# State scan in pairs of states, and a counting stage with the additions first

## What is computed

```python
e = leaky_relu(s_src[src] + s_tgt[tgt], 0.2)          # attention logits, one per edge and head
attn = exp(e - max(e)) / segment_sum(...)[tgt]
agg = segment_sum(proj[src] * attn, tgt)              # sum over a node's edges
deg = segment_sum(ones, src)                          # how often a node is a source
perm = argsort(deg + deg_noise)                       # order of the nodes in the scan
# state scan over the permuted nodes, 16 states per feature:
h = dA_t * h + dBx_t                                  # dA = exp(dt * A), dBx = dt * x * B_t
y_t = h @ C_t                                         # summed over the 16 states
```

## Time and profile before

| | |
|---|---|
| median of 3 runs | 4070.81 us (4067.91 to 4075.13) |
| the profiled execution | 4066.82 us |
| its span, first to last instruction | 4065.2 us |
| mean granted clock of TensorE | 0.864 |
| counting stage, edge pairs 0 to 35 | from 211 to 560 us |
| state scan, 28 chunks | from 1063 to 3112 us |

### The profile page before, as it was taken

The page is one execution under the profiler, slowest core; times in us unless marked ns, Lnnn a source line. Parts: engine busy times, 40 slices in busy tenths (PEclk is TensorE's granted clock), DMA queues, the critical chain, the costliest instruction groups (busy, mean ns, idle before and its releaser), DMA issues. The chain is left out here.

```text
span 4065.2 us, 65532 instructions
## 1 busy us (share of the span) xinstructions
PE 3029.7 (75%) x17084; PEld 2263.6 (56%) x17085; DVE 2844.4 (70%) x5471; ACT 1949.6 (48%) x4229; POOL 2414.6 (59%) x2259
## 2 busy tenths in 40 slices
PE   5356665672778888787887887888875689839998
PEld 4245554551556565565655655656554355438887
DVE  4455558992698988989989899898996588611111
ACT  2111122230666667666666666666764466512222
POOL 4465555567666666666666666666665467534443
PEclk8666676775889999999999999999998899969999
DMA  4332243445444444444444444444446334236665
GB/s 151 103 82 66 66 120 97 106 118 171 121 117 117 114 119 114 116 114 118 116 113 117 115 113 118 116 112 119 114 117 137 71 86 105 74 120 143 144 141 108
DMA packets 284690, 460.34 MB, mean 113 GB/s; under 512 B 57719, under 2 KB 203624, under 8 KB 284168
## 3 DMA queue, kind: packets, MB, share of 16 engines
q0 software_dynamic: 121472, 292.57, 29.8%
q1 hardware_dynamic: 162952, 165.07, 14.3%
HBM read 394.01 MB, written 63.44 MB: 113 GB/s over the span
## 5 line engine op out<-in xcount | busy, mean ns | idle before, releaser
L498 POOL DMA_INDIRECT el_g<-table,el_ix x1344 | 1344.0, 1000 | 699.0 <-issue 373.2
L616 PE MATMUL fl_ps<-el_g,el_oh 128*128 128x260 f32 x3520 | 1082.6, 461 | 405.9 <-DVE ACC L551 394.8
L616 PEld LDWEIGHTS fl_ps<-el_g,el_oh 128*128 128x128 f32 x3520 | 781.7, 230 | 756.3 <-issue 598.1
L498 POOL DMA_INDIRECT el_g<-table,eg_src x436 | 503.1, 1154 | 336.0 <-PE fl_ps L616 188.4
L1036 DVE TENSOR_TENSOR_SCAN mb_h<-mb_dA,mb_h,mb_dB 128x224 f32<-128x224 f32 x896 | 572.0, 670 | 12.9 <-issue 12.9
L565 ACT ACTIVATE el_oht<-el_away 128x512 bf16<-128x512 bf16 x445 | 280.3, 630 | 593.4 <-PE fl_px L604 573.4
L541 DVE TENSOR_TENSOR el_g<-el_g,fl_pw 128x1024 f32<-128x1024 f32 x440 | 532.8, 1211 | 0.0
L1273 PE MATMUL fl_py<-mb_hc,ident 128*128 128x448 f32 x896 | 454.0, 591 | 0.0
L559 ACT ACTIVATE el_away<-el_dst,el_less 128x512 bf16<-128x512 bf16 x445 | 319.8, 719 | 150.5 <-DMA el_dst<-dst_rows 67.0
L1163 ACT ACTIVATE mb_dA<-mb_dt,mb_a 128x224 f32<-128x224 f32 x900 | 382.2, 475 | 1.4
L1263 PE MATMUL fl_pbc<-mb_parts,mb_sel 96*128 96x224 bf16 x898 | 166.1, 268 | 253.5 <-DVE mb_hc L1045 253.5
(11 more groups left out here) (298 smaller groups left out, 4985.2 us busy)
## 6 DMA issues: line engine op xcount, KB each, us to landing
el_dst<-dst_rows SPq DMA_DIRECT2D x446, 128.0 KB, 3.1
ex_w<-in_moe_W SPq DMA_DIRECT2D x56, 512.0 KB, 3.5
el_g<-table,el_ix POOLq DMA_INDIRECT x1344
ex_x<-routed_x SPq DMA_DIRECT2D x56, 257.0 KB, 2.8
el_g<-table,eg_src POOLq DMA_INDIRECT x436
mb_x<-sorted_x SPq DMA_DIRECT2D x30, 224.0 KB
table<-px_tr POOLq DMA_DIRECT2D x49, 130.0 KB, 2.3
px_x<-in_x SPq DMA_DIRECT2D x49, 128.0 KB, 3.2
```

Of the source, the lines that this page charges most:

```text
L498: pool.indirect_dma_start(out=G[b // GU][:, b % GU * NJ + j, :], out_offset=None, in_=dram["table"], in_offset=bass.IndirectOffsetOnAxis(a ...
L616: mm = nc.tensor.matmul(pS, OH[:, n % (2 * GU), j, :], G[n // GU % 2][:, n % GU * NJ + j, :], start=j == 0, stop=j == NJ - 1)
```

## The change

In the state scan two states go together. A pair of states has one `scan` over four rows (two states, two halves) of 225 elements: the arrays `dA`, `dB` and `H` get a column in front of each row. In that column `dA` is zero and `dB` holds the carried state, so that the scan, which runs over all 900 elements as one row, starts anew at each of them. ScalarE's `keep_last` writes the last column of H to `H0` and copies the next pair's carried state into dB's front column. `inflow` and `read_out` are 896 wide. `dB` and `H` have one buffer for a pair instead of two for single states, B and C have one PSUM buffer each for a pair. The scan of a pair stands in the even slot, its read-out in the odd slot, and so does the inflow of the next pair; on TensorE `copies_c` stands in the even slot, `copies_b` in the odd one, and `sum_up` of both states of the pair before in the even slot behind the edge work. ScalarE's `keep_last` stands in the odd slot behind the one-hots. `give_out` on VectorE moves from slot 1 to slot 2.

In the counting stage a slot of VectorE does add, mark_low, scale, mark_high. The even and odd columns of a block are multiplied together: 23 matmuls of 128 by 196 for a block instead of 46 of 98 by 64, and two matmuls at the end pick and add the two wanted quarters.

The diff, cut to its core:

```diff
+
+                def mark_high(c):
                     two = HI[:, c * DB:(c + 1) * DB].rearrange("p (e u) -> p e u", u=2)
-                    nc.vector.tensor_tensor(HA[:, c % 2], two.unsqueeze(2).to_broadcast([P, DB // 2, SRC_HI, 2]),
+                    nc.vector.tensor_tensor(HB[:, c % 2], two.unsqueeze(2).to_broadcast([P, DB // 2, SRC_HI, 2]),
                                             REP[:].unsqueeze(1).to_broadcast([P, DB // 2, SRC_HI, 2]), ALU.is_equal
-                                            ).then_inc(split_hot, 1)
-
-                def mark_low(c):
-                    two = LO[:, c * DB:(c + 1) * DB].rearrange("p (e u) -> p e u", u=2)
-                    nc.vector.tensor_tensor(HB[:, c % 2], two.unsqueeze(2).to_broadcast([P, DB // 2, SRC_LO, 2]),
-                                            REP[:, 0:SRC_LO, :].unsqueeze(1).to_broadcast([P, DB // 2, SRC_LO, 2]), ALU.is_equal
                                             ).then_inc(split_hot, 1)
                 for q in range(G_COUNT):
                     S = pair(q)
                     steps = logits(dve, S) if q % GU == 0 else None
+                    if q >= 3:
+                        add(dve, S - 3)
                     if steps:
                         next(steps)
                     if q < ND:
-                        mark_high(q)
+                        mark_low(q)
                     if steps:
                         next(steps)
                         next(steps)
-                    if q >= 3:
-                        add(dve, S - 3)
-                    if steps:
                         next(steps)
                         next(steps)
                     if q >= 1:
                         scale(dve, S - 1)
                     if q < ND:
-                        mark_low(q)
+                        mark_high(q)
                 dve.wait_ge(counted, ND)
+                nc.vector.tensor_copy(BOTH[:], both[:]).then_inc(both_sb, 1)
+                dve.wait_ge(summed_up, 1)
                 nc.vector.tensor_tensor(key[:], count[:], noise[:], ALU.add).then_inc(keyed, 1)
...
                         pe.wait_ge(split_hot, 2 * c + 2)
-                        for e in range(DB):
-                            mm = nc.tensor.matmul(count[:], HA[:, c % 2, e // 2, :, e % 2], HB[:, c % 2, e // 2, :, e % 2], start=c == 0 and e == 0,
-                                                  stop=c == ND - 1 and e == DB - 1, skip_group_check=True)
+                        for e in range(DB // 2):
+                            mm = nc.tensor.matmul(both[:].rearrange("p v u -> p (v u)"), HA[:, c % 2, e].rearrange("p v u -> p (v u)"),
+                                                  HB[:, c % 2, e].rearrange("p v u -> p (v u)"), start=c == 0 and e == 0,
+                                                  stop=c == ND - 1 and e == DB // 2 - 1)
                         mm.then_inc(counted, 1)
+                pe.wait_ge(both_sb, 1)
+                for u in range(2):
+                    mm = nc.tensor.matmul(count[:], BOTH[:, :, u], PICK[:, u, :], start=u == 0, stop=u == 1)
+                mm.then_inc(summed_up, 1)
         nc.all_engine_barrier()
...
-            dB, H, HC = (sb(f"mb_{n}", [P, 2, KD, TC]) for n in ("dB", "h", "hc"))
+            dA = sb("mb_dA", [P, 4, KD, 1 + TC])
+            dB, H = (sb(f"mb_{n}", [P, 2, KD, 1 + TC]) for n in ("dB", "h"))
+            HC = sb("mb_hc", [P, 2, 2, KD, TC])
             taps = dA[:].rearrange("p b k t -> p (b k t)")[:, 0:CONV * D].rearrange("p (j d) -> p j d", j=CONV)
-            XN = [t[:].rearrange("p b k t -> p (b k t)")[:, u * D:(u + 1) * D] for t in (dB, H, HC) for u in range(3)]
-            H0 = sb("mb_h0", [P, KD, NS])
...
+            H0, ZERO = sb("mb_h0", [P, N2, 2, KD]), sb("mb_zero", [P, 1])
             Y, O, OR = sb("mb_y", [P, KD, TC]), sb("mb_o", [P, KD, TC]), sb("mb_or", [RB, TS, D])
-            pBC = [ps(f"fl_pbc{b}", [P, 2, TC]) for b in range(2)]
+            pB, pC = ps("fl_pb", [P, 2, TC]), ps("fl_pc", [P, 2, TC])
             pY, pM = ps("fl_py", [P, KD, TC]), ps("fl_pm", [P, 512])
             wide = lambda t: t[:, 0:KD * TC].rearrange("p (k t) -> p k t", k=KD)
             xs = dram["sorted_x"].rearrange("(c r p) d -> c p r d", p=RB, r=TS)
...
                     m, n = p.number, p.n
-                    dve.wait_ge(s["BC"], m + 1)
-                    if not early(m, 2):
-
-                        dve.wait_ge(s["h"], (m - 1) * KD)
-                    nc.vector.tensor_tensor(dB[:, n % 2], U[:, n // NS % 2], pBC[n % 2][:, 0, :].unsqueeze(1).to_broadcast([P, KD, TC]),
-                                            ALU.mult).then_inc(s["dB"], 1)
-
-                def scan(p, k):
+                    dve.wait_ge(s["B"], m + 1)
+                    if not early(m, 1):
+
+                        dve.wait_ge(s["h"], m)
+                    wide_u = U[:, n // N2 % 2].unsqueeze(1).to_broadcast([P, 2, KD, TC])
+                    nc.vector.tensor_tensor(dB[:, :, :, 1:], wide_u, pB[:].unsqueeze(2).to_broadcast([P, 2, KD, TC]), ALU.mult
+                                            ).then_inc(s["dB"], 1)
+
+                def scan(p):
+
                     m, n = p.number, p.n
-                    if k == 0:
-                        dve.wait_ge(s["dB"], m + 1)
-                        dve.wait_ge(s["dA"], m + 1)
-                        if not early(m, 2):
-
-                            dve.wait_ge(s["h0"], m - 1)
-                    nc.vector.tensor_tensor_scan(H[:, n % 2, k, :], dA[:, n % 4, k, :], dB[:, n % 2, k, :],
-                                                 H0[:, k, n % NS:n % NS + 1], ALU.mult, ALU.add).then_inc(s["h"], 1)
+                    dve.wait_ge(s["dB"], m + 1)
+                    dve.wait_ge(s["dA"], 2 * m + 2)
+                    if not early(m, 1):
+
+                        dve.wait_ge(s["h0"], 2 * m)
+                        dve.wait_ge(s["hc"], m)
+                    line = lambda t: t.rearrange("p s k t -> p (s k t)")
+                    nc.vector.tensor_tensor_scan(line(H[:]), line(dA[:, n % 2 * 2:n % 2 * 2 + 2]), line(dB[:]), ZERO[:, 0:1],
+                                                 ALU.mult, ALU.add).then_inc(s["h"], 1)
                 def read_out(p):
                     m, n = p.number, p.n
-                    dve.wait_ge(s["h"], (m + 1) * KD)
+                    dve.wait_ge(s["h"], m + 1)
+                    dve.wait_ge(s["C"], m + 1)
                     if not early(m, 2):
                         dve.wait_ge(s["y"], m - 1)
-                    nc.vector.tensor_tensor(HC[:, n % 2], H[:, n % 2], pBC[n % 2][:, 1, :].unsqueeze(1).to_broadcast([P, KD, TC]),
-                                            ALU.mult).then_inc(s["hc"], 1)
+                    nc.vector.tensor_tensor(HC[:, n % 2], H[:, :, :, 1:], pC[:].unsqueeze(2).to_broadcast([P, 2, KD, TC]), ALU.mult
+                                            ).then_inc(s["hc"], 1)
                 def prepare(c, b, at):
...
@@ -1100,18 +1126,18 @@
                 def slot(M, S):
                     n, c = M.n, M.of(NS)
                     at, b = n % NS, n // NS % 2
-                    if at == 1 and not early(c, 1):
+                    two = two_states(M)
+                    if at == 2 and not early(c, 1):
                         give_out(c - 1, 1 - b)
-                    if not early(M.number, 1):
-                        read_out(M - 1)
                     steps = logits(dve, S) if S and S.n % GU == 0 else None
                     if steps:
                         next(steps)
-                    scan(M, 0)
+                    if at % 2:
+                        read_out(two)
+                    else:
+                        scan(two)
                     if steps:
                         next(steps)
-                    scan(M, 1)
-                    if steps:
                         next(steps)
                     if S:
                         add(dve, S - 3)
@@ -1121,7 +1147,8 @@
                     if S:
                         scale(dve, S - 1)
                     prepare(c + 1, 1 - b, at)
-                    inflow(M + 1)
+                    if at % 2:
+                        inflow(two + 1)
                 for k in range(SCAT):
                     edges_vector(dve, pair(G_RANK + k))
...
                     for at in range(k * NS // PREP, (k + 1) * NS // PREP):
                         prepare(0, 0, at)
-                inflow(Slot(0, 0))
+                inflow(two_states(Slot(0, 0)))
+                nc.vector.memset(dB[:, :, :, 0:1], 0.0).then_inc(s["set"], 1)
+                dve.wait_ge(s["set"], 13)
...
                     m, n = p.number, p.n
-                    act.wait_ge(s["h"], (m + 1) * KD)
-                    nc.scalar.copy(H0[:, :, n % NS], H[:, n % 2, :, TC - 1]).then_inc(s["h0"], 1)
+                    act.wait_ge(s["h"], m + 1)
+                    nc.scalar.copy(H0[:, n % N2], H[:, :, :, TC]).then_inc(s["h0"], 1)
```

(70 more changed lines are left out.)

33 lines of the change are left out of this document (22 added, 11 removed).

## The result

| | before | after |
|---|---|---|
| median | 4070.21 us (4 runs) | 4258.77 us (4255.71 to 4261.82, 4 runs) |
| span of the profiled execution | 4065.2 us | 4256.0 us |
| mean granted clock | 0.864 | 0.841 |
| counting stage ends (memset of the rank stage) | 568.8 | 510.2 |
| first to last inflow of the state scan | 2047.1 us | 2294.3 us |

The change made the kernel slower: ratio 1.0462, 95% interval 1.0443 to 1.048. The direction was right; at 4165 us (3960 to 4220) the loss was too small, and the time lies 39 us above the range. The counting stage gave 58.5 us where I had 76, and the scan stretch lost 247 where I had 175; the other stages differ by 2.

What follows compares the result with a forecast made beforehand. No engine was full: in the scan TensorE paced 22.6 us of each chunk and VectorE the rest, in counting their turns. 4066.8 - 76 (counting) + 175 (scan, 6.5 by 27 chunks) = 4166, given as 4165, range 3960 to 4220.

Steps and rivals of the forecast that it cites:

- Prices: VectorE instruction times in the scan: long scan 2.10 us (bounds 1.29 to 2.34), 896-wide product 1.00 us.
- Part one: Scan chunk from add of slot 1 to reduction of slot 6, TensorE setting the pace: 26.9 instead of 22.6, +4.3 us.
- clock kept: Rival: TensorE stays at 2.4 GHz in both places; chunk costs only +2.6 us, total 4061, no change; chance .12.
- Part two: Rest of the scan chunk, to the next add of slot 1: work -2.5, new waits +4.7, net +2.2 us.
- six named waits: In part two, together +4.7 us: decay .4, slot 7's add 1.2, prepare 1.7, slots 8, 11, 15 .3, .5, .6.
- lost overlap: Scan-stretch VectorE instructions right behind what they need lose .1 us each, with the logits' chain .9 a chunk.
- Counting stage: GpSimd becomes the bound, its last gather done at 484 instead of 560: -76 us (bounds -130 and -24).
- what the marks cost a turn: Delay of GpSimd's packed gathers in the counting stage: each mark_high about 1.7 us, each mark_low .85.
- more of it: Rival: low clock in slots 13 to 15 and 10, each with late inflow or scan; 9.5 a chunk, 4247; chance .12.
- One place only: Rival: TensorE's clock falls in only one of two scan places; 4.5 us a chunk, 4113; chance .18.
- TensorE keeps ahead: Rival: TensorE's chain does not end last, VectorE alone paces; scan gains 2.0 a chunk, 3937 in all; chance .20.
- my likeliest: The main forecast for the whole kernel, 4165 us; alone it has 4110 to 4215; chance .38.

Runs made afterwards that it cites:

- unedited kernel: The changed kernel without any edit, as control for the edited ones: 4253.65 us, ratio 1.0448 to the kernel before in session A.
- three edits: Changed kernel with B copies behind C copies, even slots' add ahead of the scan, add's register load ahead of the logits: 4071.51 us, ratio 0.9995 (A).
- A: Session in which the kernel before takes 4072 us; the result's 4070 is like it.
- C: Three sessions in which the kernel before takes 4732 to 4738 us; the unedited changed kernel has 4480.75 us, ratio 0.948.
- B: Session in which the kernel before takes 4633 us; counting part alone 0.968, scan part alone 0.987.
- the split: Convolution's 16 matmuls laid half in slot 3, half in slot 4; on top of the three edits, ratio 0.915 to 0.917 to the kernel before (C).

## Why the prediction was wrong, by its own steps

**Prices: right.** The long scan has a record of 2.09 and a pace of 2.00 (2082.36 to 2084.36) against my 2.10, the wide product 1.08 and 1.00. By the means of the profile's page (2092 - 670) / (900 - 224) is 2.10 ns a further element, where I had extrapolated 2.35 and settled near it. The Trainium skill's half throughput ("DVE: opcode table, instruction layouts, handler registers and perf-mode slots", section "Datapath and trigger behaviour"), with the 0.96 GHz of its "Trainium Kernel Development and Optimization", is by estimate 2.08 ns an element and 1.99 for the scan; the trace's 2.00 agrees. VectorE's work a chunk fell by 2.3 (16.83 + 48.34 to 17.32 + 45.55) against 2.0.

**Part one: right in size and in the late add; what it said of the clock held only in part.** +4.3 was forecast, +4.0 measured (22.6 to 26.6). The add of slot 2 came 6.48 behind that of slot 1 (forecast 6.58), the gather sums 7.03 (7.15) and 3.80 long (3.6). With slow sums part one is 27.2, without 24.8. That is 2.4 in 20 of 27 chunks, 1.8 a chunk, as in the prediction. The rival *clock kept* had +2.4 for this part, and the 7 chunks with fast sums show +2.2. But the prediction made a pause of 4.3 ahead of these sums the cause of the lower clock. The pause was 1.8 to 4.0 (2.95 above), and in 10 of 26 chunks the granted clock had already fallen to 0.5 before it, 1.7 to 1.9 us behind slot 1's add, while slot 1's sums ran behind a pause of 2.5 to 3.0. In the 7 chunks with fast sums it was slot 1's sums that ran slow (3.83) behind a pause of 4.1 to 4.5, and the clock was back at 1.0 for slot 2's. That the average came out right is to that extent luck.

**Part two: this step failed,** +2.2 forecast, +4.9 measured (50.7 to 55.6). Its six named waits sum to 4.7 as forecast (decay .47, add of slot 7 1.04, prepare 1.66, slot 8 .33, slot 11 .79, slot 15 .43) and the work fell by 2.8 instead of 2.5. What failed is the list: VectorE's gaps grew by 7.7, from 2.3 to 10.0. The 3.0 that are missing are small and sit everywhere: the register load ahead of the add in three logits slots (.71 each instead of .25, 1.35), the three scans right behind their inflow (.22 each, .66), the scan of slot 0 (.57, of which .46 is a wait for its decay and the rest the loop's edge), one more late add (.27). I had priced lost overlap at .1 an instruction and no register load at all. From 1100 to 3000 us the row of the loads is 49.1 us in the unedited kernel and 8.1 with three edits, where it stands ahead of the logits. Over 28 chunks the 2.7 are 75 us; less 10 for part one and 6 more for the chunk that I left out of 28, that is the 72 us that the stretch was longer than forecast. This term alone takes the time out of the range; with the counting stage's error alone it would have been some 4185.

**Counting stage: the mechanism right, the size off.** -76 forecast, -58.5 measured. GpSimd is the bound and issues without a break. The term that was mis-sized is what the marks cost a turn: I had 2.55, but of the stage from 213 to 501 the 147 gathers (GpSimd's group in that stretch, the row below) by 1.25 take only 184 us; 104 us are left for 34 turns, 3.1 each. Each of the 34 mark_highs catches a gather that starts right after it and lasts 3.14 to 3.25, which is 2.2 to 2.3 more than .95, where I had 1.7 on average. I had read one row of 2.92; others in the trace before took up to 3.28.

```profile
L504 POOL DMA_INDIRECT el_g<-table,eg_src x147 | 244.8, 1665 | 44.8 <-issue 44.8
```

**Sum.** 4166 + 72 (stretch) + 17.5 (counting) + 2 is 4258, the profiled execution's 4257.6 within a microsecond. The time fell near the rival *more of it* (4247), but not by its mechanism: the inflow of slot 15 waited .43. *One place only* and *TensorE keeps ahead* are refuted in A. The range's upper end was my likeliest plus little, although a list of waits can only be too short. And no case of the prediction holds for the sign in other sessions: in C, where TensorE completes late, the same change gains 5.2%.

## What to carry to other kernels

When two steps are fused, ask first what stands behind the longer instruction: here an add of .4 us that frees another engine's PSUM bank stood behind a scan of 2.1, and moving it ahead gave 147 us, of 182 that the three edits gave together. A wait that is taken away alone moves to the next instruction of that engine (162 us of inflow waits went, 4 us came back); take a wait away only with what is late behind it. After the large waits are listed, count the instructions whose cover the new order takes (register loads, an operation right behind what it needs): some 2 us a chunk here, all on one side.

## What the runs showed of the hardware that I had not expected

- The same kernel took 4072, 4633 and 4735 us in different sessions. In the slow ones the semaphores of TensorE's scan work rise late behind the modelled end of the matmuls: over 0.5 us in 245 of 631 (B) and 215 of 599 (C) in the old order between 1200 and 3000 us, up to 7.6, and up to 10.2 with the edits and the split; never in any of the six traces of A. The granted clock there is lower (0.85 and 0.83 against 0.93 from 1100 to 3000 us), but the changed kernel has 0.86 in A without one late rise. What halts TensorE, and whether it is the chip, is open.
- This turns the sign of a change: orders in which VectorE and TensorE take turns at each step (the old count, the old scans) lose most there. That fewer turns are the reason is argued from the stages, not shown, and the rank stage, which is the same in all kernels, is 65 to 83 us slower there too.
- The register load ahead of the add shows as .71 us of idle time where two instructions of .2 us stand before it (the changed kernel), and as .25 where a scan of .67 stands ahead of the last of these (before).
